# Dependent VectorE steps set apart in the queue, routing operands read from a bank, and queries and one decay bound on VectorE

## What is computed

```
x = x + mamba(layernorm(x))           # 32 heads of 16, state 128, conv of 4 taps
    dt = softplus(dt_in + dt_bias); A_bar = exp(-exp(A_log) * dt)
    h_t = A_bar_t h_(t-1) + dt_t B_t x_t;  y_t = C_t h_t + D x_t
    out = rmsnorm(y) * silu(z) @ Wout
x = x + cross_attention(layernorm(x), ctx)    # 16 heads of 16, key mask
    q = (x @ Wq.T + bq) / 4;  p = softmax(q k - 10000 (1 - mask))
x = x + shared_ffn(xf) + sum over the top 2 of 16 experts   # xf = layernorm(x)
    probs = softmax(xf @ Wr)
```

## Time and profile before

| | |
|---|---|
| median of three runs | 4331.63 us (4328.83 to 4337.89) |
| profiled execution | 4321.73 us, span 4320.1 us |
| busy in the span | PE 4024.4 us (93%), DVE 3366.7 (78%), ACT 2840.8 (66%), POOL 2233.6 (52%) |
| granted TensorE clock | 0.946 of 2.4 GHz in the mean |

### The profile page before, as it was taken

One profiled execution on the slowest core, in us unless ns is written; L12 is line 12 of the kernel. 1 busy time (PEld: TensorE's weight loads), 2 busy tenths in 40 slices (PEclk: granted clock), 3 DMA queues, 4 the chain that ended last, 5 costly groups with the idle time before them and its releaser, 6 DMA issues.

```text
span 4320.1 us, 118128 instructions
## 1 busy us (share of the span) xinstructions
PE 4024.4 (93%) x34582; PEld 3103.4 (72%) x34583; DVE 3366.7 (78%) x8730; ACT 2840.8 (66%) x7282; POOL 2233.6 (52%) x2996
## 2 busy tenths in 40 slices
PE   5999999999999999997997999999999999999998
PEld 4777877787788777875775666666666666666665
DVE  4888888888888888884554777878787877778776
ACT  4777877787787777774443666666565666566664
POOL 3555555555555555551223555555555555555554
PEclk9898889899999999987998999999999999999999
DMA  3333332323323323232441001010111111111110
GB/s 124 123 103 120 97 123 88 104 90 104 108 89 105 108 87 106 87 104 70 146 144 47 29 29 33 27 35 27 34 30 31 30 31 30 31 32 29 30 31 20
DMA packets 222642, 304.14 MB, mean 70 GB/s; under 512 B 57216, under 2 KB 176256, under 8 KB 222592
## 3 DMA queue, kind: packets, MB, share of 16 engines
q1 hardware_dynamic: 197632, 249.83, 18.5%
q0 software_dynamic: 19200, 52.45, 3.7%
q10 hardware_dynamic: 5760, 1.24, 0.2%
HBM read 239.18 MB, written 64.23 MB: 70 GB/s over the span
## 4 chain that ended last, share of the span: by engine, by line
PE 68%; DVE 18%; issue 8%; ACT 3%; DVEq 1%; DMA 1%; POOL 1%; ACTq 1%; POOLq 0%; SPq 0%
PE Q L1481 18%; PE Q L1474 16%; PE Q L1486 10%; PE Q L1509 4%; PE Q L1515 4%; PE Q L1845 3%; PE Q L1878 3%; PE Q L1697 3%; DVE arena L872 2%; PE Q L1524 2%; DVE arena L825 2%; PE Q L1709 2%; DVE rt L992 1%; DVE sel L977 1%; ACT arena L1196 1%
## 5 line engine op out<-in xcount | busy, mean ns | idle before, releaser
L1486 PE MATMUL Q<-ident,arena 128*128 128x128 f32 x3872 | 647.8, 290 | 119.0 <-ACT arena L1204 38.2
L1486 PEld LDWEIGHTS Q<-ident,arena 128*128 128x128 f32 x3872 | 464.1, 147 | 285.1 <-issue 138.3
L640 POOL TENSOR_TENSOR arena<-arena 128x1024 f32<-128x1024 f32 x256 | 488.7, 1924 | 69.3 <-DMA arena<-cum_rows 68.4
L1481 PE MATMUL Q<-Wkvl,arena 128*128 128x512 f32 x1024 | 499.6, 600 | 0.0
L705 POOL TENSOR_TENSOR l<-l,half_pow 128x8 f32<-128x8 f32 x192 | 318.5, 1659 | 231.1 <-DVE l L1083 229.2
L1325 ACT ACTIVATE arena<-Q,mx 128x128 f32<-128x128 f32 x1024 | 277.9, 382 | 210.3 <-DVE mx L909 210.3
L1474 PE MATMUL Q<-arena,Win 128*128 128x128 f32 x2560 | 373.9, 293 | 1.5 <-DVE arena L853 1.1
L730 POOL TENSOR_TENSOR arena<-arena,part_of 128x512 f32<-128x512 f32 x256 | 263.7, 1041 | 195.8 <-DVE part_of L1121 195.8
L1474 PEld LDWEIGHTS Q<-arena,Win 128*128 128x128 f32 x2560 | 340.1, 204 | 32.9 <-issue 25.7
L1515 PE MATMUL Q<-ident,arena 128*128 128x128 f32 x2048 | 308.9, 286 | 16.3 <-ACT arena L1325 13.4
L872 DVE TENSOR_TENSOR arena<-arena,Q 128x1024 f32<-128x1024 f32 x256 | 311.8, 1218 | 7.7 <-ACT arena L1271 7.0
(11 more groups left out here) (291 smaller groups left out, 10419.9 us busy)
## 6 DMA issues: line engine op xcount, KB each, us to landing
arena<-cum_rows SPq DMA_DIRECT2D x256, 512.0 KB, 6.5
arena<-routed_rows SPq DMA_DIRECT2D x144, 128.0 KB, 2.0
expert_rows<-arena POOLq DMA_DIRECT2D x144, 128.0 KB, 2.0
arena<-in_x_dram SPq DMA_DIRECT2D x128, 128.0 KB, 4.5
arena<-in_ctx_dram SPq DMA_DIRECT2D x128, 128.0 KB, 2.1
x_rows<-arena SPq DMA_DIRECT2D x128, 128.0 KB, 1.7
arena<-x_rows SPq DMA_DIRECT2D x128, 128.0 KB, 2.1
out_dram<-arena SPq DMA_DIRECT2D x64, 128.0 KB, 1.7
```

The lines of the kernel that those rows point to most:

```text
L640: tell(g.tensor_tensor(E8[j], E8[j], cums[:, 8 * j:8 * j + 8].unsqueeze(2).broadcast_to([P, 8, T]), ALU.subtract), "diff")
L1481: last = mm(out, lhs(c), rhs(c), start=c == 0, stop=c == n - 1)
L1486: last = nc.tensor.transpose(out[:, c * P:(c + 1) * P], src[:, c * P:(c + 1) * P], ident[:, :])
```

## The change

- `link` is joined by `cue` (issue and increment) and `heed` (wait). The dependent steps of chains M, W, F, D, V, P and G become steps of their own in ORDER, with other chains' steps between them in most places: `Mln1` and `Mln1v`, `Dsp`, `Dsr`, `Dss`, and so on. Where they stay neighbours in DVE's list (`Dss Dsz Ds7 Ds6 Ds5`) the wait is as before.
- PE writes iota as a product of a row of ones with a row of iota beside the logits in Q[7]. Line 977 reads it there and writes both masks in bf16; line 979 goes. The ranks and counts are sums of two products each, and PE adds the base to the ranks; line 990 goes, and the product with the masks reads the bank. ACT's exponentials of the logits wait for the masks.
- Queries: two scalar_tensor_tensor instructions on DVE ((q + bias) times the scaled half mask), 256 outputs each, in place of ACT's four.
- First decay group: DVE takes min(x, 0) in place (128x1024) and ACT exp(x), in place of ACT's Abs and exp(-|x|). The other three groups stay.
- New orders in phase 1 on all five queues; ACT's second softplus step is a step of its own (`Dae`). Links on DVE in phase 1: 26 in place of 28.

Of the diff, the declarations of tiles and semaphores, the setup and the link counts are left out here.

```diff
@@ -49,22 +49,22 @@
         "SP": """
-            Yc Ncb0 Mx Ncb1 Ncb2 Ncb3 Gm Ox Xm Dco Go
+            Ncb0 Yc Ncb1 Mx Ncb2 Ncb3 Gm Ox Xm Dco Go
...
         "POOL": """
-            Nd0 Nd1 Mln1 Nd2 Nd3 Wln2 Gsc Fln3 Osq Oyg Wx1r Orms
+            Nd0 Mln1 Nd1 Nd2 Nd3 Wln2 Gsc Fln3 Osq Oyg Wx1r Orms
...
         "DVE": """
-            Mln1 Wln2 Gtop Gslot Nm0 Zgz Yk Ghg Ddt Nm1 Dsp Dsp6 Dsp4 Dsp2 Gxo Dsp0 Pho Nm2 Fln3 Nm3 Vcv1 Oy Vcv2 Xm0 Xm1 Oss Vcv3 Fr Vxs2 Xm2 Xm3
-            Vxdt Bcb Ox1
+            Mln1 Gtop Mln1v Nc0 Wln2 Wln2v Gwt Gslot Gsn Nm0 Zgz Ghg Ddt Nm1 Dsp Ghh Dsr Yk Dss Dsz Ds7 Ds6 Ds5 Nm2 Ds4 Gxo Ds3 Pho Ds2 Phm Ds1 Ds0
+            Phx Dsd Fln3 Dsa Nm3 Fln3v Wq Vcv1 Oy Xm0 Xm1 Vcv2 Oss Fr Vcv3 Fri Bcb Frs Vxs2 Xm2 Xm3 Ox1 Vxdt
...
         "ACT": """
-            YcT Ne0 Pt0 Nf0 Ne1 Ztz Mln1 Nf1 Gth Mln1n Pt1 Pt2 Dab Ne2 Pt3 Wln2 Xmr POT Yv Nf2 Ne3 Wln2n Nf3 Vcv Dcum Wq Bbc Fln3 Fln3n Xm0 Xm1 Vcth
-            Frx Xm2 Xm3
+            Pt0 Ne0 Mln1 YcT Pt1 Ztz Ne1 Gth Mln1n Nf1 Dab Pt2 Dae Ne2 Pt3 Nf2 Wln2 POT Yv Ne3 Wln2n Nf3 Vcv Dcum Xmr Fln3 Fln3n Xm0 Bbc Xm1 Vcth Frx
+            Xm2 Xm3
...
         "PE": """
-            YcT Pt0 Zz Yk Yv Zzh Pt1 Ggu Gguh Mln1n Pt2 Ddt Pt3 Ppv Gdn Ppv0 Ppv1 Ppv2 Ppv3 Vip1 POT Vip1h Wln2n Nv0 Wq Dcum Nv1 Nv2 Nv3 Bbc Xs0 Fln3n
-            BCB Fr Oss Opr Xs2 Oprh VxsT Frk
+            YcT Pt0 Zz Pt1 Zzh Ggu Gguh Pt2 Mln1n Yk Ddt Pt3 Yv Vip1 Ppv Ppv0 Ppv1 Ppv2 Ppv3 Gdn POT Wln2n Vip1h Wq Dcum Nv0 Nv1 Nv2 Nv3 Xs0 Fln3n Bbc
+            Fr Oss BCB Opr Xs2 Oprh VxsT Frk
@@ -358,6 +356,18 @@
+            eng.wait_ge(SEM[f"link_{name}"], at(f"link_{name}", b, steps[name]))
+            if bare:
+                eng.sem_inc(SEM[f"passed_{eng.engine.name}"], 1)
...
+        def cue(name, ins):
...
+            steps[name] += 1
+            assert steps[name] <= links[name], name
+            ins.then_inc(SEM[f"link_{name}"], 1)
...
+        def heed(eng, name, b, bare=False):
@@ -803,44 +812,57 @@
             def M(b):
...
-                moments("ln1", xa, stM, mvM, "M_DVE", b)
+                yield from moments("ln1", xa, stM, mvM, "M_DVE", b)
             def D_(b):
-                J = lambda ins, bare=False: link(dve, "D_DVE", b, ins, bare)
+                J = lambda ins: cue("D_DVE", ins)
...
-                u = dts[:, 1, :]
+                u, s, z, tail_of = (dts[:, k, :] for k in range(1, 5))
...
+                yield "sr"
+                heed(dve, "D_DVE", b)
...
-                s, z, tail_of = dts[:, 2, :], dts[:, 3, :], dts[:, 4, :]
+                yield "ss"
+                heed(dve, "D_DVE", b)
...
+                yield "sz"
+                heed(dve, "D_DVE", b)
...
+                yield f"s{TERMS - 1}"
+                heed(dve, "D_DVE", b)
...
-                    if k % 2 == 0:
-                        yield f"sp{k}"
+                    yield f"s{k}"
+                    heed(dve, "D_DVE", b)
...
-                yield "sp0"
+                yield "s0"
+                heed(dve, "D_DVE", b)
+                J(v.scalar_tensor_tensor(tail_of, tail_of, 2.0, s, ALU.add, ALU.mult))
+                yield "sd"
+                heed(dve, "D_DVE", b)
...
-                J(v.scalar_tensor_tensor(tail_of, tail_of, 2.0, s, ALU.add, ALU.mult))
...
+                yield "sa"
+                heed(dve, "D_DVE", b)
...
             def V(b):
-                J = lambda ins, bare=False: link(dve, "V_DVE", b, ins, bare)
...
+                    else:
+                        heed(dve, "V_DVE", b)
...
-                        J(last)
+                        cue("V_DVE", last)
@@ -865,6 +887,11 @@
             def N(b):
+                for j in (0,):
+                    if j == 0:
+                        yield "c0"
+                        done(dve, "diff", b, 1)
+                        tell(v.tensor_scalar(Ew[j], Ew[j], 0.0, None, ALU.min), "cap")
@@ -899,7 +926,16 @@
             def W(b):
                 yield "ln2"
...
-                moments("ln2", x1, stX, mvX, "W_DVE", b)
+                yield from moments("ln2", x1, stX, mvX, "W_DVE", b)
+                yield "q"
+                done(dve, "q0", b)
+                was(dve, "S0", b, 4)
+                src = cut(Q[2][:, D:2 * D], DC)
+                dst = QT0.rearrange("p (c k) q -> p c k q", k=2)
+                for c in range(DC):
+                    last = v.scalar_tensor_tensor(dst[:, c, :, :], src[:, c, :].unsqueeze(1).broadcast_to([P, 2, T]), bqk0[:, 0, c:c + 1],
+                                                  par[:, :].unsqueeze(2).broadcast_to([P, 2, T]), ALU.add, ALU.mult)
+                tell(last, "q0c")
             def X(b):
@@ -912,8 +948,12 @@
                 yield "ho"
...
-                link(dve, "P_DVE", b, v.reciprocal(rc0[:, :].unsqueeze(2), pv[:, :, AW:AW + 1]))
-                link(dve, "P_DVE", b, v.tensor_tensor(pv[:, :, 0:AW], pv[:, :, 0:AW], rc0[:, :].unsqueeze(2).broadcast_to([P, AH, AW]), ALU.mult))
+                cue("P_DVE", v.reciprocal(rc0[:, :].unsqueeze(2), pv[:, :, AW:AW + 1]))
+                yield "hm"
+                heed(dve, "P_DVE", b)
+                cue("P_DVE", v.tensor_tensor(pv[:, :, 0:AW], pv[:, :, 0:AW], rc0[:, :].unsqueeze(2).broadcast_to([P, AH, AW]), ALU.mult))
+                yield "hx"
+                heed(dve, "P_DVE", b)
@@ -962,34 +1002,39 @@
             def F(b):
-                J = lambda ins, bare=False: link(dve, "F_DVE", b, ins, bare)
                 yield "ln3"
...
-                moments("ln3", x2, stF, mvF, "F_DVE", b)
+                yield from moments("ln3", x2, stF, mvF, "F_DVE", b)
                 yield "r"
...
-                J(v.max(top, logits), bare=True)
-                J(v.max_index(rti[:, 0, :], top, logits))
-                tell(v.tensor_scalar(rt[:, 0, 0:1], top[:, 0:1], -1.0, None, ALU.mult), "rmax")
+                cue("F_DVE", v.max(top, logits))
+                yield "ri"
+                heed(dve, "F_DVE", b, bare=True)
+                cue("F_DVE", v.max_index(rti[:, 0, :], top, logits))
+                yield "rs"
+                heed(dve, "F_DVE", b)
+                v.tensor_scalar(rt[:, 0, 0:1], top[:, 0:1], -1.0, None, ALU.mult)
...
-                    last = v.scalar_tensor_tensor(sel[:, k, :], iota[:, :], rti[:, 0, k:k + 1], ones[:, 0:NE], ALU.is_equal, ALU.mult)
-                J(last)
-                tell(v.tensor_tensor(selb[:, :], sel[:, 0, :], sel[:, 1, :], ALU.add), "sel")
+                    last = v.scalar_tensor_tensor(sel[:, k, :], Q[7][:, D + 2 * NE:D + 3 * NE], rti[:, 0, k:k + 1], ones[:, 0:NE], ALU.is_equal, ALU.mult)
+                tell(last, "sel")
             def G(b):
-                J = lambda ins, bare=False: link(dve, "G_DVE", b, ins, bare)
+                J = lambda ins: cue("G_DVE", ins)
                 yield "top"
...
+                yield "wt"
+                heed(dve, "G_DVE", b)
...
                 yield "slot"
...
-                J(v.tensor_tensor(rt[:, 7, :], Q[7][:, D:D + NE], base[:, :], ALU.add))
...
-                J(v.tensor_tensor(rt[:, 8:10, :], sel[:, :, :], rt[:, 7, :].unsqueeze(1).broadcast_to([P, 2, NE]), ALU.mult))
+                J(v.tensor_tensor(rt[:, 8:10, :], sel[:, :, :], Q[7][:, D:D + NE].unsqueeze(1).broadcast_to([P, 2, NE]), ALU.mult))
+                yield "sn"
+                heed(dve, "G_DVE", b)
...
                     tell(v.tensor_reduce(meta[:, 0:2], rt[:, 8:10, :], AX.X, ALU.add), "slot")
@@ -1231,6 +1278,7 @@
+                yield "ae"
@@ -1264,28 +1312,25 @@
             def N(b):
...
-                done(act, "diff", b, 1)
-                tell(s_.activation(Ew[0], Ew[0], ACT.Abs), "gap")
-                yield "f0"
-                done(act, "gap", b, 1)
-                tell(s_.activation(Ew[0], Ew[0], ACT.Exp, scale=-1.0), "E")
+                done(act, "cap", b, 1)
+                tell(s_.activation(Ew[0], Ew[0], ACT.Exp), "E")
...
-                done(act, "gap", b, 2)
+                done(act, "gap", b, 1)
...
-                done(act, "gap", b, 3)
+                done(act, "gap", b, 2)
...
-                done(act, "gap", b, 4)
+                done(act, "gap", b, 3)
...
             def Y(b):
@@ -1302,15 +1347,6 @@
                 yield "ln2n"
...
-                yield "q"
-                done(act, "q0", b)
-                was(act, "S0", b, 4)
-                src = cut(Q[2][:, D:2 * D], DC)
-                dst = QT0.rearrange("p (c k) q -> p c k q", k=2)
-                for k in range(2):
-                    for c in range(DC):
-                        last = s_.activation(dst[:, c, k, :], src[:, c, :], ACT.Identity, bias=bq0s[:, c, k:k + 1], scale=par[:, k:k + 1])
-                tell(last, "q0c")
             def X(b):
@@ -1338,7 +1374,7 @@
-                done(act, "rmax", b)
+                done(act, "sel", b)
@@ -1659,12 +1695,18 @@
                 yield "r"
                 done(pe, "ln3_T", b)
```

(12 more changed lines are left out.)

25 lines of the change are left out of this document (12 added, 13 removed).

## The result

The changed kernel takes 4097.97 us (median of 4 runs, 4094.73 to 4099.57). The kernel before, beside it, takes 4334.76 us (median of 4, 4328.83 to 4346.76). The ratio is 0.9449, with the interval [0.9427, 0.9472]: 237 us less. The profiled execution took 4099.57 us (span 4097.9); the mean granted clock over the span is 0.980, before it was 0.946.

A forecast was written before the change was run, and what follows sets the result against it. It took PE, slowed by clock drops, to bound the first phase; 62 x 1.55 = 96 us off the profiled 4321.73 gave 4226, plus 9.9 for the median 4236. Forecast 4190 to 4270 (0.50), whole range 4140 to 4300.

The forecast's parts named there:

- What bounds the kernel: First phase: PE nearest to full, 28.1 us of a 30.25 us body; a clock drop costs 2.7 to 3.9 us.
- The clock's share: First-phase bodies: 40% at full clock, 60% of the second kind, mean 28.7 us, 1.55 us less a body.
- PE at full clock: PE in full-clock bodies: 26.0 plus 0.6 us for six more issues, 26.6; with 0.5 of waits a body takes 27.1.
- Operands from the bank: L977 and L992 on DVE: reading the bank ends hold-ups beside POOL's subtractions, 2.9 us of DVE a body.
- Steps apart: DVE's dependent steps separated by other chains' steps: 19 x 0.115 = 2.2 us of DVE saved.
- Queries and bound on DVE: Work moved from ACT to DVE: 0.8 us more for the queries and 0.8 for the bound; ACT isn't the bound.
- Order: PE's queue: B/C projection fills the 0.25 us wait, CB product the 0.34; of 1.5 us of waits 0.5 stays.
- The clock stays up: Rival: with the gaps filled PE no longer drops, 27.1 us for all bodies, 195 us less, about 4137; chance 0.22.
- The bound meets POOL: Rival: DVE's new tensor_scalar and a POOL subtraction hold each other, 59 of the 96 us lost, 4295; chance 0.04.
- Softplus late: Rival: DVE's softplus ends some 2 us later, PE waits for it and drops in every body, 4410; chance 0.05.
- Only the hazards: Rival: clock keeps its shares or PE waits as before, 0.5 to 1.0 us a body, 4270 to 4300; chance 0.14.
- The change doesn't do what it says: Rival: hold-ups aren't operand reads, 2.9 us stay on DVE, gain under 0.2%, about 4330; chance 0.05.

The follow-up runs named there:

- e1: Changed kernel with the B/C projection and the product of C and B back at their old places in PE's and ACT's queues: 4322.59 us.
- e11: Kernel of e8 with DVE's first two score maxima moved ahead of the convolution's second step: 4240.09 us, ratio 0.9779.
- e8: Kernel before with only the B/C projection, its ACT copy and the product of C and B moved to their new places: 4309.71 us.
- n0: Changed kernel without POOL's scatter; SP writes the rows to fixed places, phase 2 reads fixed rows: 4087.66 us.
- e10: Changed kernel without PE's matmuls for iota and base; masks read iota in SBUF, DVE adds the base: 4086.45 us.
- c2: Kernel of e10 repeated on another chip: 4125.78 us, with the changed kernel beside it at 4100.52.
- e2: Changed kernel with masks reading iota in SBUF and the slot product reading an SBUF copy of the ranks: 4100.62 us.
- e7: Kernel before with the routing part alone: bf16 masks from the bank, iota and base by matmul, product from the bank: 4350.3 us.
- e3: Changed kernel with DVE's dependent steps put straight behind the ones they read again: 4242.54 us, ratio 0.9791.
- n3: Kernel of e3 without POOL's scatter; SP writes the rows to fixed places, phase 2 reads fixed rows: 4169.42 us.
- e5: Changed kernel with the queries written by ACT's four activations again in place of DVE's two products: 4144.72 us.
- e6: Changed kernel with the first decay group bounded by ACT's Abs again and DVE's tensor_scalar gone: 4188.17 us.
- n6: Kernel of e6 without POOL's scatter; SP writes the rows to fixed places, phase 2 reads fixed rows: 4116.23 us.

## Why the prediction was wrong

- **What bounds the kernel: right.** PE, by the clock in its thin stretch. e1 and e11 show it: e1 differs from the changed kernel in the place of two groups, e11 from e8 in the place of one step of DVE, which takes one wait of PE away.
- **The clock's share, the step that failed**: "The 16-column and one-column matmuls stay together, so they won't vanish: I take 40% at full clock and 60% of the second kind". It is 5 of 60, 8%. By the prediction's own 27.1 and 29.8 that makes 27.33 us a body, 62 x 1.37 = 85 us of the 138 us by which it missed. The thin matmuls did stay, and grew by two issues. I weighed the length of the thin run (2.1 us to 1.5) and took it that each wait filled brings its part; e8 against the changed kernel, and e11 against e8, show that whether the stretch has any wait left matters more than its length. The drop body's 29.93 us for 29.8 is partly luck: PE's busy time in it is 28.17 (forecast 29.3, of 29.8 less 0.5 of waits), and a wait of 1.3 to 1.5 us of ACT beside the scatter is in it. In n0, without the scatter, the four such bodies at 0.88 take 28.45.
- **PE at full clock, mis-sized**: 25.58 for 26.6. The issues cost what I took or more: without four of them PE is at 24.78 in e10 and at 25.04 in c2, 0.5 to 0.8 less. Left out was that the four value groups now run as one train, 64 issues in 2.14 us (1014.14 to 1016.28). Before, they took 0.65, 1.27 for two together, and 0.65, so 0.4 us more. The rest of the difference I did not trace to its lines. Waits are 0.84 in place of 0.5. Together: 26.42 for 27.1 at full clock.
- **The sum again.** Both together are 28.7 - 26.71 = 2.0 us, and 62 of that are 123 us. The rest is 15: I put 9.9 on for the step from the profiled execution to the median, where that of after is 1.6 above its median, and 3 or 4 lie outside the 60 bodies, where the span fell by 10 us and two bodies' worth is 7.
- **Operands from the bank: right in size, wrong in worth.** 2.8 us left DVE, and by e2 their return costs nothing, and by e7 their going alone, with PE's six issues, loses 15 us. DVE was busy longer than PE in only 6 of the 18 bodies at full clock. In the changed kernel it is at 23.4, 2.2 below PE, either way. SBUF — State Buffer, section Who interferes with whom, in the Trainium skill, has the rule for the mask (601 ns with SBUF operands, 225 from the bank); the product needs no bank in the new order, where it begins just ahead of the subtraction.
- **Steps apart: right in kind.** DVE's busy time went down by less (23.4 for 22.3), and e3 shows a worth of 145 us that isn't its 1.3 us of DVE: 63 us of it is when the values end against the scatter, and most of the rest is PE waiting for the queries on DVE (62 x 1.05 = 65 us by n3). The prediction had named that last wait, but not what keeps it away.
- **Queries and bound on DVE: I costed them and gave them no gain.** Their going back costs 47 and 90 us (e5, e6), since ACT stood in PE's way: for the mask's row, and for the values' turn beside the scatter. "ACT isn't the bound" was read from its busy time; what counts is what is behind it in its queue.
- **Order.** The move of the B/C projection was priced as two waits filled, 0.6 us. It is worth 225 us where all else is in place (e1), and 24 us alone (e8). The projection and the product were always moved together.
- **The rivals.** The clock stays up, at 4137, was the nearest, and 0.22 was too little for it. The bound meets POOL: it holds one small operation for 0.4 us a body and meets no subtraction, and the change isn't slower. Softplus late: PE waits for L851 in 7 instances, 2.0 us in all (0.27 in the body at 1144), and the change is not slower. Only the hazards: the clock's shares did not stay, and e7 and e2 exclude it. The change doesn't do what it says: excluded, 110 of 128 masks run beside a subtraction and take 225 ns.

**Left open.** How much of the 225 us is the projection and how much the product. Which of e7's two sides, less work on DVE or more thin issues on PE, brings the drop into every body. Why PE's signal reaches ACT only 0.5 us after POOL's second issue: that the wait hangs on the scatter is shown by n3 and n6, the way inside the chip isn't, nor why e1 escapes it (below). 29 us of e6 and some 17 of e3. And the same kernel (e10, c2) differs by 39 us between two chips, where the kernel before differs by 10.

## What to carry to other kernels

Look at the granted clock by the microsecond, find what TensorE does just before it falls, and put dense work with its inputs long ready before and between the thin matmuls, in the same order change; then look whether any wait is left in that stretch, since one of 1.1 us undid most of it (e8 gains 24 us, e11 98). Undo each part of a change alone and in its surroundings: here the part with the largest saving of busy time was worth nothing in the new order, and the reordering of two groups nearly everything, but only with the rest in place. An engine that isn't the bound by its busy time can still be by what stands behind it in its queue.

## What the runs showed of the hardware that I had not expected

- A signal of TensorE to ACT, given while POOL issues the first of two indirect DMAs, can arrive only 0.51 us after the second issue ends: 1009.31 to 1009.82 in e3, 1011.55 to 1012.10 (0.55) in e6, 1171.08 to 1171.59 after. ACT lost 1.71, 1.30 and 1.31 us by it. Given as the first issue starts (1009.56 against 1009.54, after) it is in time. That it falls into the first issue isn't enough, though: in e1 the values end 0.15 to 0.97 us into it in 53 of 60 bodies, and ACT copies without a wait in all of them, as it does in the three drop bodies of e2. In the one below they end at 193.00, 0.91 us into an issue that ends at 193.15. What else it takes isn't known.

```profile
191.92 1.08 PE L1560 MATMUL Q<-arena 128*17 128x128 f32 x32
192.09 1.06 POOL L679 DMA_INDIRECT routed_rows<-arena,meta  x1 [0.57 <-DVE arena L1047]
193.46 0.96 POOL L679 DMA_INDIRECT routed_rows<-arena,meta  x1 [0.30 <-issue]
193.62 0.59 ACT L1368 ACTIVATE arena<-Q 128x512 f32<-128x512 f32 x1
```

- TensorE's clock can fall with hardly any wait about. In e1 the drop comes in 54 bodies of 60 though PE is busy 29.27 of 30.35 us; the only waits about it are 0.25 us before the fall and 0.34 after it, beside matmuls of 16 columns and of one. The Trainium skill, TensorE: Matmul & The Clock Gate, section Part 1, ties the clock to how busy the array has been shortly before. These runs agree with that in direction (e11, with one wait less than e8, has 42 bodies at 1.00 for 16), but PE's busy time in the profile doesn't tell when the clock falls.
- An edit that takes 2.6 us a body from DVE and gives PE six thin issues (e7) left 59 of 60 bodies at 0.89, where 42 of 60 were below full before; without four of these issues (e10, c2) none is below full.
